# Dispatch weights of four token tiles turned by one transposition, and a spreading product that contracts over 32 partitions instead of 128

## The reference, cut to what matters

```python
logits = jnp.einsum('bsd,de->bse', x, gate_w) + gate_b
probs = jax.nn.softmax(logits, axis=-1)
top_probs, top_idx = jax.lax.top_k(probs, 2)
top_probs = top_probs / jnp.sum(top_probs, axis=-1, keepdims=True)
dispatch = jnp.sum(one_hot(top_idx, 16) * top_probs[..., None], axis=-2)   # [tokens, 16]
hidden = jax.nn.silu(x @ w1[e]) * (x @ w2[e])                              # every expert e
expert_out = hidden @ w3[e]
y = sum over e of expert_out * dispatch[:, e]
```

## Time and profile before

| | us |
|---|---|
| median of 3 runs (lowest 4076.63, highest 4082.5) | 4076.75 |
| the profiled execution's own time | 4094.36 |
| its span, from the first to the last instruction | 4092.5 |
| TensorE busy | 3528.9 |
| VectorE busy | 3082.9 |
| ScalarE busy | 2406.3 |
| GpSimd busy | 1995.2 |

### The profile page before, as it was taken

How to read it: one execution, slowest core, us unless ns; L and a number is a source line. 1 busy time by engine, 2 the same in 40 slices (tenths; PEclk the granted TensorE clock), 3 DMA queues, 4 the chain that set the end, 5 groups by cost and what they waited for, 6 DMA issues and landing times.

```text
span 4092.5 us, 58291 instructions
## 1 busy us (share of the span) xinstructions
PE 3528.9 (86%) x21688; PEld 1903.8 (47%) x21688; DVE 3082.9 (75%) x4896; ACT 2406.3 (59%) x4152; POOL 1995.2 (49%) x1805
## 2 busy tenths in 40 slices
PE   5979997999899999999999999999899989956332
PEld 2434444454545445454545445454545455535322
DVE  6456577986699687987799688977698678875775
ACT  5745774577656775577656775577556775532111
POOL 0000064664456363664466364655466464667572
PEclk8979997999899998999899999999899989965555
DMA  4000122232222231231222232232222322244472
GB/s 114 1 8 1 40 77 66 79 97 61 74 79 86 76 97 53 81 102 55 72 84 85 77 91 66 77 97 60 73 81 79 81 83 65 85 115 123 101 171 62
DMA packets 374827, 314.91 MB, mean 77 GB/s; under 512 B 312689, under 2 KB 317041, under 8 KB 374545
## 3 DMA queue, kind: packets, MB, share of 16 engines
q0 software_dynamic: 85248, 231.33, 19.1%
q1 hardware_dynamic: 289296, 79.88, 9.1%
HBM read 279.30 MB, written 57.69 MB: 82 GB/s over the span
## 4 chain that ended last, share of the span: by engine, by line
PE 68%; DVE 12%; ACT 8%; DVEq 4%; issue 3%; POOL 3%; SPq 1%; DMA 0%; POOLq 0%; ACTq 0%
PE PS L1605 62%; PE PS L1815 3%; POOL G L457 3%; PE PS L1641 2%; DVEq L497 2%; DVE G L495 2%; DVE work L923 2%; DVE G L501 1%; ACT work L1410 1%; DVE small L909 1%; ACT small L1455 1%; ACT xn_hl L1323 1%; PE PS L1645 1%; DVE work L823 1%; DVE st L463 1%
## 5 line engine op out<-in xcount | busy, mean ns | idle before, releaser
L457 POOL DMA_INDIRECT G<-corner_table,index x1800 | 1994.6, 1108 | 1986.2 <-DVE values L503 695.6
L1605 PE MATMUL PS<-xn_hl,w 128*128 128x512 f16 (+2 forms) x3584 | 814.3, 356 | 61.3 <-DVE work L923 52.9
L1410 ACT ACTIVATE work<-PS 128x768 f32<-128x768 f32 (+2 forms) x800 | 651.9, 823 | 279.2 <-PE PS L1605 230.1
L1482 ACT ACTIVATE work<-PS,descale 128x512 f32<-128x512 f32 (+2 forms) x896 | 567.0, 633 | 417.0 <-PE PS L1605 404.0
L823 DVE TENSOR_TENSOR work<-work 128x768 f32<-128x768 f32 (+2 forms) x496 | 480.0, 972 | 303.8 <-PE PS L1605 254.7
L923 DVE SCALAR_TENSOR_TENSOR work<-PS,descale,work 128x512 f32<-128x512 f32 (+2 forms) x896 | 602.3, 678 | 132.5 <-ACT work L1482 124.0
L1605 PE MATMUL PS<-work,xm 128*64 128x400 f32 (+3 forms) x3200 | 623.0, 502 | 0.0
L495 DVE TENSOR_TENSOR G<-G,corner_w 128x768 f32<-128x768 f32 x600 | 561.1, 950 | 59.4 <-DMA G<-corner_table,index 58.1
L1605 PE MATMUL PS<-xn_hl,xn_hh 128*128 128x384 f16 (+2 forms) x1600 | 545.7, 341 | 47.1 <-ACT work L1410 38.6
L1605 PE MATMUL PS<-xn_hl,xn_ll 128*128 128x384 f16 (+2 forms) x1600 | 540.8, 338 | 0.0
L1605 PEld LDWEIGHTS PS<-xn_hl,w 128*128 128x128 f16 x3584 | 338.0, 100 | 298.4 <-DVE work L923 87.4
(11 more groups left out here) (256 smaller groups left out, 4156.0 us busy)
## 6 DMA issues: line engine op xcount, KB each, us to landing
G<-corner_table,index POOLq DMA_INDIRECT x1800
corner_table<-rows_scratch SPq DMA_DIRECT2D x32, 784.0 KB
corner_table<-G SPq DMA_DIRECT2D x8, 841.0 KB, 8.5
xin<-x SPq DMA_DIRECT2D x8, 768.0 KB, 5.7
rows_scratch<-xln SPq DMA_DIRECT2D x8, 768.0 KB
x_scratch<-xB SPq DMA_DIRECT2D x8, 768.0 KB
yw_scratch<-yw SPq DMA_DIRECT2D x7, 784.0 KB, 6.5
x<-x_scratch SPq DMA_DIRECT2D x3, 784.0 KB, 6.2
```

Of the source, the lines that this page charges most:

```text
L457: GP.indirect_dma_start(G[0:rows, n % 2, tap * 4 * C:(tap + 1) * 4 * C], None, tables[b % 2], bass.IndirectOffsetOnAxis(ap=index[0:rows, c ...
L1410: A.activation(relu[0:rows, u % 2, :, 0:n], PS[u % 2][0:rows, :, 0:n], ACT.Relu).then_inc(s["relu_done"], 1)
L1482: A.activation(silu[:, e % 2, 0:w], S[e % 2][:, 0:w], ACT.Silu, scale=descale[:, MOE1:MOE1 + 1]).then_inc(s["silu_done"], 1)
L1605: return P.matmul(o, a, b, start=start, stop=stop, skip_group_check=True)
```

## The change

The weights of tiles t, t+7, t+14 and t+21 are put side by side in `dsplit`, so that 128 columns belong to four tiles and one product with the identity turns them all. The result has group g of 7 tiles (that is, chunks 2g and 2g+1) on partitions 32g to 32g+31. Two banks take all of it: one for the even chunks, one for the odd ones. The spread for chunk c reads only the 32 partitions of group c//2, for the moving and for the stationary operand, of which there are now four copies.

```diff
-        dT = xn_hh
+        dT = xn_hh[:, 0:2 * 512].rearrange("p (q n) -> p q n", q=2)
...
-        dsplit = sb("dsplit", [TP, T, 2 * E], f16)
+        dsplit = sb("dsplit", [TP, 7, 4 * 2 * E], f16)
+        ds_v = dsplit[:, :, :].rearrange("p i (g x) -> p g i x", g=4)
+        disp_v = small[:, 4, 0:28 * E].rearrange("p (g i e) -> p g i e", g=4, i=7)
...
+        def share_rows(c):
+
+            return slice(c // 2 * 2 * E, (c // 2 + 1) * 2 * E)
...
-            sp.dma_start(stage3[0:2 * E, 1536:1536 + E * C], pick_in).then_inc(s["w_staged"], 16)
+            for g in range(4):
+                sp.dma_start(stage3[g * 2 * E:(g + 1) * 2 * E, 1536:1536 + E * C], pick_in).then_inc(s["w_staged"], 16)
...
-                V.tensor_copy(dsplit[:, :, 0:E], disp[:, :, :])
-                dve.drain()
-                V.tensor_tensor(dsplit[:, :, E:2 * E], disp[:, :, :], dsplit[:, :, 0:E], ALU.subtract).then_inc(s["disp_split"], 1)
+                V.tensor_copy(ds_v[:, :, :, 0:E], disp_v)
+                dve.drain()
+                V.tensor_tensor(ds_v[:, :, :, E:2 * E], disp_v, ds_v[:, :, :, 0:E], ALU.subtract).then_inc(s["disp_split"], 1)
...
+            V.memset(small[:, 4, :], 0.0)
...
-            V.memset(pick[:, :], 0.0)
-            dve.wait_ge(s["w_staged"], 16 * 15)
+            dve.wait_ge(s["w_staged"], 16 * 18)
...
-            V.tensor_copy(pick[0:2 * E, :], stage3[0:2 * E, 1536:1536 + E * C])
+            V.tensor_copy(pick[:, :], stage3[:, 1536:1536 + E * C])
...
-                for c in range(NCH):
-                    act.wait_ge(s["disp_tr"], k * NCH + c + 1)
-                    A.activation(dT[0:2 * E, span(c)], S[c % 4][0:2 * E, 0:width(c)], ACT.Copy).then_inc(s["disp_cm"], 1)
+                for q in range(2):
+                    rows, n = share_rows(NCH - 1 - q).stop, width(q)
+                    act.wait_ge(s["disp_tr"], 2 * k + q + 1)
+                    A.activation(dT[0:rows, q, 0:n], S[3 - 2 * q][0:rows, 0:n], ACT.Copy).then_inc(s["disp_cm"], 1)
...
-                mm(Y1[:, 0:width(c)], pick[:, p * 128:(p + 1) * 128], dT[:, span(c)]).then_inc(s["share_done"], 1)
+                r = share_rows(c)
+                mm(Y1[:, 0:width(c)], pick[r, p * 128:(p + 1) * 128], dT[r, c % 2, 0:width(c)]).then_inc(s["share_done"], 1)
...
-                for c in range(NCH):
-                    if c >= 4:
-                        pe.wait_ge(s["disp_cm"], k * NCH + c - 3)
-                    for i, t in enumerate(tiles_of(c)):
-                        rows = tile_rows(t)
-                        ins = mm(S[c % 4][0:2 * E, i * TP:i * TP + rows], dsplit[0:rows, t, :], ident16[0:rows, 0:rows])
+                for q in range(2):
+                    bank = S[3 - 2 * q]
+                    for i in range(4 - q):
+                        rows = (4 if q == 0 and i < 3 else 3) * 2 * E
+                        ins = mm(bank[0:rows, i * TP:(i + 1) * TP], dsplit[:, 4 * q + i, 0:rows], ident16[:, :])
+                    if q == 0:
+                        r = share_rows(NCH - 1)
+                        ins = mm(bank[r, 3 * TP:3 * TP + REM], dsplit[0:REM, 3, r], ident16[0:REM, 0:REM])
                     ins.then_inc(s["disp_tr"], 1)
-                pe.wait_ge(s["disp_cm"], (k + 1) * NCH)
                 up(0, 0)
+                pe.wait_ge(s["disp_cm"], 2 * (k + 1))
                 up(1, 0)
```

## The result

The changed kernel takes 4110.08 us (median of 6 runs, 4105.75 to 4114.27) where the kernel before takes 4081.56 (6 runs, 4076.63 to 4091.15): ratio 1.0067, 95% interval 1.0054 to 1.0080, slower by 28.5 us. The prediction had 4106 us, +29 on the median it knew.

The account below looks back on a forecast made before the run. TensorE bounds the kernel, VectorE nearly full in the experts. Hand-over -22.2, start +1.3 and spreads +50 give +29 us on the 4076.75 median: 4106 us, slower by 0.7%; 8-in-10 range 4074 to 4122.

Parts of the forecast that it names:

- price of a 32-row spread: TensorE, spread to `collect`: shape change 0.09 us plus uncovered weight load 0.055, so 0.145 us for each of 448 spreads.
- of 65 us shows: Expert stages: of 65 us more TensorE time, 50 us lengthen the run; bounds 36 to 65.
- image 0's experts: Experts of image 0: VectorE has slack there, so all 56 pairs' price counts, 8.1 us.
- hand-over: Gate to experts: fewer turns and copies, `up(0, 0)` not waiting for copies; -22.2 us over eight images, bounds 18 to 27.
- start: Program start: three more `pick` loads in SyncE's queue delay VectorE's first work on the weights, +1.3 us.
- sum: Whole kernel: -22.2 for the hand-over, +1.3 for the start, +50 for the spreads, together +29 us.
- rival A: Spread to `collect`: no price for the 32-partition product, shorter hand-over remains; -21 us, 4056 us; chance 0.16.
- The cover: Experts of images 1 to 7: TensorE's waits for VectorE hide part of the price; 42.3 us still show.
- I let each wait take up the delay of one pair: Images 1 to 7: 100 waits for VectorE each hide one pair's 0.145 us, leaving 292 of 392 pairs, 42.3 us.
- Rival B: Images 1 to 7: VectorE is the bound, covering most of the price; -1 us, 4076 us; chance 0.16 including nearby cases.
- 2 x 3.4: Hand-over of images 3 and 4, whose experts begin at half clock: VectorE's idle time before `hid` regained, 3.4 us each.

Follow-up runs that it names:

- experiment 6: Kernel before, each spread cut into two products of 64 columns over all 128 rows: 4091.89 us, ratio 1.0023.
- Experiments 1 to 3: Three runs: experiment 1 (changed kernel, full-row spread, ratio 0.9966), and experiments 2 and 3 (kernel before, spread over 32 or 64 rows, ratios 1.0110 and 1.0106).
- experiments 7 and 8: Kernel before, VectorE relieved of weighing and first sum for 48 of 64 convolution channels: 3997.52 us; same with 32-row spreads: 4048.53 us; one execution each.
- experiment 1: Changed kernel with the spread contracting over all 128 partitions again, `pick` as four matrices with zeros outside each group's rows: 4072.14 us, ratio 0.9966.
- experiments 2 and 3: Kernel before with only the spread's line changed, to contract over 32 rows (4129.67 us, ratio 1.0110) or 64 rows (4128.23 us, ratio 1.0106).
- experiments 1 and 9: experiment 1, and that kernel with a separate semaphore for the `pick_in` loads and its casts moved to ScalarE: 4063.08 us, ratio 0.9960.
- experiment 5: experiment 1 with one 512 KB DMA reading `pick_in` four times instead of four loads: 4075.45 us, ratio 0.9979.

## Why the prediction was right, point by point

| step of the prediction | said | measured |
|---|---|---|
| price of a 32-row spread | 0.145 us | 0.144 |
| of 65 us shows | 50 | 44.9 |
| image 0's experts | +8.1 | +7.2 |
| hand-over | -22.2 | -19.7 |
| start | +1.3 | +1.6 |
| sum | +29 | +26.8; medians +28.5 |

The hand-over is measured from first turn to first `hid`, the stages from the first silu on. Up to the silu the hand-over gained 20.5, so without this overlap the sum is +26.0. That the forecast met the medians to half a microsecond is luck: two terms were off in opposite directions, by 5.1 and 2.5 us, and the interval of the measured difference is itself 22 to 33 us. The mechanism is not luck: what 32 rows cost, what hides part of it, and which path the hand-over takes were each read rightly from rows and found again.

**The price** was right in both terms, the change of shape (0.09; 89 ns) and the uncovered load of the float32 transpose's weights (0.055), and right in treating rows like columns (experiment 6). Experiments 1 to 3 settle rival A: full rows take the price away, 32 rows alone bring it, and the 0.06 us per spread at which the net would be zero was passed by far.

**The cover** was somewhat larger than said. The step that was mis-sized is "I let each wait take up the delay of one pair": images 1 to 7 lost 37.7 us and not 42.3, so 100 waits took up 18.7 us, 0.19 each, more than one pair's 0.144. TensorE's waits for `hid` over the run say the same, before and here:

```profile
PE PS L1613 <- DVE work L930: 37.2, 68, 1.4
```

They fell from 52.9 us in 109 waits to 37.2 in 68: 15.7 us went there, of the 19.6 that did not show (64.5 - 44.9). Where the other 4 went was not found. Image 0 was taken "in full", and lost 7.2 of 8.1. Rival B put the bound on VectorE in images 1 to 7; experiments 7 and 8 show the mechanism to be real, but relieving VectorE brings back only 12.3 of the 56.4 us of these images' price (49.6 - 37.3), and even at full load two thirds of the price show. Its own sign would have been image 2's experts under 205 us; they took 208.3.

**The hand-over** was right for images 0 and 1 (2.72 us each, said 2.7) and for image 2 (2.56, said 2.5), with the path named: the read of the feed-forward banks sets the time. In images 0 and 1 the prediction has 2.8 from the first turn on, less 0.1 for the longer writes of `dsplit`; these don't take longer (0.39 + 0.63 us, before 0.57 + 0.57). Mis-sized was "2 x 3.4" for images 3 and 4. It gave back all of VectorE's idle time before `hid`, as if the read set the time there too. At half clock it doesn't: image 3 of the changed kernel begins at half clock like before, and VectorE, done with the read, still waits for the silu:

```profile
1577.99 0.75 DVE L930 SCALAR_TENSOR_TENSOR work<-PS,descale,work 128x512 f32<-128x512 f32 x1 [0.78 <-ACT work L1489]
```

From first turn to first `hid` it gained 2.6 us, no more than image 2. A gain of 3.4 needs an image that begins at half clock before and at full clock after. In the profiled executions image 4 gained 3.0, and images 6 and 7 only 1.7, since they began at full clock before and at half clock after. In experiment 1, with the same hand-over and the last five images all at full clock, the sum is 21.9 us. So how much of the 22 is seen depends on the clock at which each image begins; one execution of each kernel cannot tell whether the change itself moves that clock.

**What stays open.** The stages add up to +26.8 us, the two spans differ by 16.8, the medians by 28.5. The rest lies between one expert stage and the next. Windows there, the changed kernel after images 2 and 3:

```profile
1330.80:1577.30 246.50, 227.12 (x1578) 125.20 (x1577) 178.12 (x270) 177.95 (x309) 124.94 (x110) 0.94 0.29 80
1785.50:2040.40 254.90, 235.54 (x1578) 131.27 (x1577) 177.89 (x270) 178.48 (x308) 123.36 (x110) 0.90 0.29 77
```

The same work takes 246.5 us at a mean clock of 0.94 and 254.9 at 0.90. In the profiled execution of before, which was 12.8 us above the median of its six runs (the changed kernel's was 1.1 above), the stretches after images 1 to 6 took 250.8 to 256.4, longer hand-over included. The one-execution comparison has this noise, the medians less, and the medians agree with the sum by stages within their interval. The way to the first turn varies too: it begins at 243.4 us before and at 240.1 and 239.3 in experiments 2 and 3, whose start is unchanged. What decides in which image the clock falls was not found. For the same reason I leave open why the medians of experiments 1 and 9 (-11.2 and -15.5 us) show less than their hand-over and start would give, -21.9 + 4.1 = -17.8 and -22.0 + 0.2 = -21.8: the first lies within its interval, the second just beyond the end of its own (-21.2).

## What to carry to other kernels

Here a matmul that contracts over fewer rows than its neighbours saved no time on TensorE by that, and paid for the change on each side that wasn't one already: read the price from any place in the trace where shapes meet, and multiply by the count before anything else. Zeros in the unused rows keep the shape and cost TensorE nothing; here that one line makes nearly all of the difference between 1.0067 and 0.9966. A saving of 20 us in eight places is soon eaten by a seventh of a microsecond in 448.

## What the runs showed of the hardware

64 rows, 32 rows and 64 columns cost nearly the same beside products of 128 by 128: 84 to 91 ns at the change behind the spread and 55 ns more at the float32 transpose that follows, whose weights then load beside it and not under the spread, at the 2.4 GHz level. Where the spread had the reduced shape of the `w3s` product before it, the step between the two was 103 ns shorter (experiment 6, 422 instead of 525). Not expected was the load of experiment 5: one DMA of 512 KB that reads its source four times was in 9.8 us after its issue, with the 16 DMA engines busy for 0.22 of the time; four of 128 KB were in within 4.2 us, with the engines busy for 0.85.
